# Draining three pending output groups per step instead of two in the feed-forward loop

## What is computed

```
xn = layernorm(x)
h  = float2fix(xn @ w1 + b1)            # 1024 -> 4096, rounded to multiples of 1/256
h  = pwlin_gelu(h); h = float2fix(h)
ffn = float2fix(h @ w2 + b2)            # 4096 -> 1024
x  = x + attention(xn) + ffn            # latent attention, 16 heads, causal, rotary part of 32
```

## Time and profile before

| | us |
|---|---|
| median of 3 runs | 4835.5 (4832.95 to 4841.89) |
| the profiled execution | 4835.37 |
| its span, core 7 (the slowest) | 4833.5 |
| spans of the eight cores | 4802.6 to 4833.5 |
| feed-forward loop, first `fh` to last `fh` | 1034.7 to 2491.4 |

### The profile page before, as it was taken

One profiled execution on the slowest core, in us unless ns is written; L12 is line 12 of the kernel. 1 busy time (PEld: TensorE's weight loads), 2 busy tenths in 40 slices (PEclk: granted clock), 3 DMA queues, 4 the chain that ended last, 5 costly groups with the idle time before them and its releaser, 6 DMA issues.

```text
span 4833.5 us, 37107 instructions; the slowest of 8 cores (4802.6 to 4833.5 us)
## 1 busy us (share of the span) xinstructions
PE 2052.4 (42%) x7072; PEld 826.9 (17%) x7072; DVE 2456.5 (51%) x4454; ACT 1140.2 (24%) x1957; POOL 388.3 (8%) x352
## 2 busy tenths in 40 slices
PE   0111016125544444444445544554544545455545
PEld 0000002001111111111111222222222222222222
DVE  2222222028876766776760666655555555555541
ACT  1111101001111111111110333433333333333320
POOL 1000000002222222222220000000000000000001
PEclk8555558656677767677765666666666666666668
DMA  5222320762232232322323444444444444444454
GB/s 98 59 52 59 91 76 13 87 84 56 52 70 70 70 70 69 74 71 68 74 64 75 80 83 83 80 75 77 75 77 80 77 78 77 78 76 78 80 94 65
DMA packets 883113, 352.69 MB, mean 73 GB/s; under 512 B 831824, under 2 KB 834384, under 8 KB 882384
## 3 DMA queue, kind: packets, MB, share of 16 engines
q1 hardware_dynamic: 871184, 309.89, 30.4%
q0 software_dynamic: 11712, 40.44, 6.3%
HBM read 174.68 MB, written 41.94 MB: 45 GB/s over the span
## 4 chain that ended last, share of the span: by engine, by line
DMA 32%; PE 23%; DVE 20%; issue 11%; ACT 6%; another core or an unknown queue 3%; SPq 2%; DVEq 1%; ACTq 0%; POOL 0%; POOLq 0%
DMA PT<-Ebuf 9%; PE ps L659 8%; DMA W1C<-w1bf 7%; DMA W2C<-w2bf 7%; DVE u_t L917 6%; PE ps L998 5%; PE ps L631 3%; DMA xtile<-xb 3%; PE ps L874 2%; ACT Ebuf L904 2%; DVE Ebuf L948 2%; PE ps L809 2%; DMA out<-OB 2%; PE ps L496 1%
## 5 line engine op out<-in xcount | busy, mean ns | idle before, releaser
L917 DVE TENSOR_REDUCE u_t<-Ebuf 128x1 f32<-128x1536 bf16 (+3 forms) x480 | 644.8, 1355 | 340.8 <-ACT Ebuf L904 339.4
L659 PE MATMUL ps<-xnTq,W1C 128*128 128x512 bf16 x1024 | 433.3, 599 | 805.2 <-DMA W1C<-w1bf 805.2
L904 ACT ACTIVATE Ebuf<-ps 128x1536 bf16<-128x1536 f32 (+3 forms) x480 | 545.1, 1137 | 943.2 <-DVE ps L892 813.4
L874 PE MATMUL ps<-kasm,qh 96*128 96x512 bf16 (+1 forms) x1152 | 449.9, 503 | 621.9 <-ACT Ebuf L904 601.5
L998 PE MATMUL ps<-PT,vtok 128*64 128x256 bf16 x2304 | 456.1, 384 | 341.3 <-DMA PT<-Ebuf 337.6
L998 PEld LDWEIGHTS ps<-PT,vtok 128*64 128x64 bf16 x2304 | 353.3, 159 | 488.5 <-issue 429.2
L631 PE MATMUL ps<-W2C,HQ 128*128 128x512 bf16 x1024 | 348.5, 493 | 177.1 <-DVE FT L607 87.1
L675 ACT ACTIVATE FT<-ps,b1t 128x512 f32<-128x512 f32 x128 | 88.2, 689 | 1251.7 <-PE ps L659 1251.7
L892 DVE TENSOR_TENSOR ps<-ps,m12sb 128x128 f32<-128x128 f32 x512 | 124.0, 288 | 378.2 <-PE ps L874 378.2
L659 PEld LDWEIGHTS ps<-xnTq,W1C 128*128 128x128 bf16 x1024 | 128.9, 135 | 1079.5 <-issue 1072.1
L874 PEld LDWEIGHTS ps<-kasm,qh 96*128 96x128 bf16 x1152 | 97.8, 108 | 924.3 <-issue 907.2
(11 more groups left out here) (93 smaller groups left out, 2189.0 us busy)
## 6 DMA issues: line engine op xcount, KB each, us to landing
W2C<-w2bf SPq DMA_DIRECT2D x256, 256.0 KB, 2.7
W1C<-w1bf SPq DMA_DIRECT2D x128, 256.0 KB, 3.3
xtile<-xb SPq DMA_DIRECT2D x32, 512.0 KB, 4.7
xtile<-xq SPq DMA_DIRECT2D x16, 512.0 KB, 4.1
out<-xtile SPq DMA_DIRECT2D x16, 512.0 KB, 3.1
w1bf<-w POOLq DMA_DIRECT2D x8, 1024.0 KB, 48.2
w2bf<-w POOLq DMA_DIRECT2D x8, 1024.0 KB, 120.6
out<-FT POOLq DMA_DIRECT2D x16, 512.0 KB, 5.8
```

Of the source, the lines that this page charges most:

```text
L659: ins = e.matmul(bkh, W1C[:, fc % 2, dc, :], XNQ[:, dc, tg * 512:(tg + 1) * 512], start=(dc == 0), stop=(dc == 7))
L874: ins = e.matmul(PS[:, (tb + m) * 512:(tb + m) * 512 + wd], QH[0:96, hp, oi * 128:(oi + 1) * 128], KA[0:96, hp, gs + m * 512:gs + m * 512 ...
L904: return e.activation(EB[:, slotE, gs:gs + gl], PS[:, tb * 512:tb * 512 + gl], AF.Exp, scale=SCALE96, accum_out=u_t[:, ub + gi:ub + gi + 1])
L917: ub=ub, gi=gi: e.reduce_max(u_t[:, ub + 3 + gi:ub + 4 + gi], EB[:, slotE, gs:gs + gl], axis=AX.X)),
```

## The change

`drain_o` may take three pending output groups per step where it took two. Nothing else differs.

```
             ev("tensor", fh, waits=whl, incs=[(s_hmm, 1)])
-            drain_o(2)
+            drain_o(3)
             if fc + 2 < 32:
                 w1_load(fc + 2)
```

## The result

The changed kernel takes 4930.62 us (median of 8 runs, 4918.12 to 4936.85) against 4834.63 (8 runs, 4826.31 to 4841.89): a ratio of 1.0196, 95% interval 1.0182 to 1.021. It is 96 us slower; the prediction was 4923 us, in a range of 4870 to 4950. The profiled execution took 4935.14 us with a span of 4933.3 on core 5, 99.8 us longer than the span before.

What follows compares the result with a forecast made beforehand. Taken as the bound: fh waiting for a W1C load queued on SP behind the drain's W2C loads. Each of three groups grows 29.1 us (16.7 exposed foq, 12.4 steady steps), +87 on 4835.5: 4923 us, range 4870 to 4950.

Steps and rivals of the forecast that it cites:

- The sign named in advance: In the changed kernel's trace, about 40 more fo's would be released by a W2C landing.
- The price of the third fo: In three-fo steps, one more W2C landing of 2.68 us, as in the tail: 11.54 becomes 14.22 us.
- Which wait makes it: On SP's queue, each W2C load waits for every earlier W2C load to have landed, by `(s_w2l, s_w2l.n)`.
- The one-fo steps: In groups 1 to 3, steps with one fo take 9.75 us as in group 0, bounds 9.1 to 10.0.
- Steps 0 and 11: In groups 1 to 3, fh stands behind an fo blocked by foq: steps 0 to 2 42.3 us, 11 to 12 31.7.
- the exposed foq: At steps 0 and 11, fh no longer slips in during foq: 16.7 us of each group's 29.1 us loss.
- The clock: In three-fo steps, fh stays at 3.57 us, the lower clock of 1.2 GHz, as TensorE idles some 4.4 us before it.
- The free third fo: Rival: in three-fo steps, SP's W2C link costs nothing, 39 steps lose 2.68 us each: 4818 us, chance 0.05.
- fh at full rate: Rival: in three-fo steps, a denser drain speeds fh up, 1.68 us less in 39 steps: 4857 us, chance 0.05.
- the covered foq: Rival: at steps 0 and 11, fh(1) and fh(12) aren't held up, 16.7 us less per group: 4873 us, chance 0.06.
- no effect: Rival: in the drain, more than two fo are never pending, so nothing happens: 4835 us, chance 0.03.

Runs made afterwards that it cites:

- the two moves of the W1C load: W1C load written ahead of the drain, against the kernel before: 4591.29 us (0.953) with three per drain, 4565.72 us (0.9474) with two.
- the third buffer: Three per drain, W2C given a third buffer with its own semaphore, loads three entries ahead, against the kernel before: 4714.01 us, ratio 0.9776.
- own-semaphore runs: A semaphore for each W2C buffer, against the kernel before: 4833.57 us (1.0025) with three per drain, 4686.64 us (0.9716) with two.
- the kernel with two per drain: The kernel before, drain of two, with the W1C load written ahead of the drain: 4565.72 us, ratio 0.9474.

## Why the prediction was right

**Direction and size.** 4923 us was forecast and 4930.62 measured, +87 against +96. Its working is borne out by segment, here per group in us, with the mean of the changed kernel's groups (core 5):

| steps | forecast | measured |
|---|---|---|
| 0 to 2 | 42.3 | 43.5 |
| 2 to 10 | 113.8 | 115.8 |
| 10 to 11 | 11.5 | 11.5 |
| 11 to 12 | 31.7 | 31.3 |
| 12 to 16 | 56.9 | 58.6 |
| 16 to 30 | 136.5 | 138.0 |
| 30 to the next 0 | 23.2 | 23.4 |
| sum | 415.9 | 422.0 |

The total is nearer than the working deserves. In the two profiled executions the groups 1 to 3, from the first to the last mark, grew from 1140.1 to 1246.1 us, 106 where 87 were forecast. What lies ahead of group 1 holds the same work and came out 5.5 us shorter, and the medians lie 96 us apart where the two profiled spans lie 99.8 apart. That part is luck. The sign named in advance, about 40 more fo's released by a W2C landing, came as 72 against 32.

**The price of the third fo**, one landing of 2.68 us from the tail, was the term that came out too small: three-fo steps are 14.5 us (the 36 steps from 2 to 10 and 12 to 16 of the three groups take 347.3+175.8 = 523.1 us), so the third fo costs 3.0. That is 0.3 us in 39 steps, 12 of the 18 us by which the three groups' sum fell short. The landings account for it. The 41 that stand in the chain of three-fo steps in groups 1 and 2 took 2.76 us in the mean (2.44 to 4.28, median 2.59), where 24 of the kernel before in its two-fo steps took 2.61 and the nine of the stretch of the earlier trace rows none over 2.7. The second landing adds its 2.76 and the 0.12 us to the next issue, and the first is 0.15 longer than it was: 3.0. That the price is a landing, and that it lies in front of fh by way of SP's queue, is shown by the two moves of the W1C load and the third buffer.

**Which wait makes it** I had put on `(s_w2l, s_w2l.n)` above all. The own-semaphore runs show that this was half of the reasoning only: with that wait gone the third fo still costs 13.2-10.2 = 3.0 us, because of the two buffers.

**The one-fo steps** were taken at group 0's 9.75 and are 9.86 (413.9 us in 42).

**Steps 0 and 11.** 42.3 and 31.7 were forecast, and 43.5 and 31.3 came. At step 0 of group 1 the W1C load beside foq's transfer took 5.33 us to land where 4.8 had been taken. That the exposed foq are 50 us of the loss was worked out before the result, and stopping the drain there gave 46 back.

**The clock.** fh was left at 3.57 us in three-fo steps and shows 3.22 to 3.57. In the window of steps 2 to 10 of group 1 the granted clock was 0.72, against 0.74 with two fo: no gain. TensorE still idled 5.2 to 7.3 us in front of fh, more than the 4.4 worked out in advance.

```profile
1389.00:1505.00 116.00, 52.41 (x160) 17.90 (x159) 63.26 (x88) 15.27 (x24) 20.20 (x16) 0.72 0.28 73
```

**The rivals.** The free third fo (4818), fh at full rate (4857), the covered foq (4873) and no effect (4835) all lie outside what was measured.

## What to carry to other kernels

When work is moved between the steps of a loop, read the step time for each amount per step out of the trace first, and don't continue it in a straight line. Here the trace before had one and two fo per step, at 9.75 and 11.5 us; three and four then came at 14.5 and 17.7. A schedule that has the same sum but is less even pays for that curve. What the next fo costs was told by the chain (one more landing) and not by the step from one to two. Read what stands behind the moved work on every in-order queue, as half of this loss was an fh behind a blocked fo and the other half a load behind other loads. And a step that is longer than its busiest engine says that something waits for a load issued too late: moving one load ahead of the drain was worth 254 us, more than any choice of how many to drain.

## What the runs showed of the hardware

A W2C load of 256 KB took 2.4 to 2.7 us to land in the stretch of the tail that the earlier trace rows spans, and up to 4.3 in the three-fo steps; beside the transfer out of foq it took 4.81. Moving the loads also moved TensorE's clock without any more matmuls: with the W1C load ahead, an fh of 8 matmuls took 1.89 us, at 2.4 GHz, where the earlier trace rows has 3.57 at 1.2. The window above shows a granted clock of 0.96, where the earlier trace rows has 0.74, and the page of that kernel has TensorE idle for 250.3 us in front of fh, against 805.2. This fh started with no wait (timeline of the kernel with two per drain):

```profile
1404.01 1.89 PE L659 MATMUL ps<-xnTq,W1C 128*128 128x512 bf16 x8
```

The Trainium skill ("TensorE: Matmul & The Clock Gate", Loop structure matters more than you think) has as its rule that waits for a DMA between matmuls lose the full rate, and the trace agrees, by the two pairs of numbers above.

The new bound has slack of its own. On VectorE the same instruction, L691 over 128x512, took 1.49 us while GpSimd's L724 was running and 0.41 when GpSimd was idle (timeline of the same kernel); whether the one causes the other was not tried:

```profile
1403.41 1.27 POOL L724 TENSOR_TENSOR FT<-FT 128x512 f32<-128x512 f32 x1
1403.47 1.49 DVE L691 TENSOR_SCALAR FT<-FT 128x512 f32<-128x512 f32 x1
...
1413.31 0.41 DVE L691 TENSOR_SCALAR FT<-FT 128x512 f32<-128x512 f32 x1
```
